# Two large groups of SBUF buffers begin at multiples of 2048 bytes instead of 64-byte ones

## What is computed

```python
def L0(x, d_list, U, Vt, weight, filt, bias):        # U = Vt = adj
    scale = jnp.sum(d_list * filt * d_list, axis=0)
    return U @ (scale[:, None] * (Vt @ (x @ weight))) + bias
def message(X, A, W):
    deg = jnp.sum(A, axis=1, keepdims=True)
    return (A / jnp.where(deg > 0, deg, 1.0)) @ X @ W
def L1(X, A, W_in, W_out):
    return message(X, A, W_in) + message(X, A.T, W_out)
x = layernorm(x + L0(x, ...adj, adj...))
x = layernorm(x + L1(x, adj, W_in, W_out))
```

## Time and profile before

| | |
|---|---|
| median of 3 runs | 762.05 us (761.66 to 762.28) |
| the profiled execution, device time | 761.1 us |
| its span, first to last instruction | 759.3 us |
| granted TensorE clock, mean over the span | 0.997 of full |
| PE busy | 743.7 us (98%), 3346 matmuls |
| DVE busy | 551.8 us (73%) |
| ACT busy | 475.5 us (63%) |
| transferred | 208.64 MB, mean 275 GB/s |

### The profile page before, as it was taken

The page is one execution under the profiler, slowest core; times in us unless marked ns, Lnnn a source line. Parts: engine busy times, 40 slices in busy tenths (PEclk is TensorE's granted clock), DMA queues, the critical chain, the costliest instruction groups (busy, mean ns, idle before and its releaser), DMA issues. The chain is left out here.

```text
span 759.3 us, 9063 instructions
## 1 busy us (share of the span) xinstructions
PE 743.7 (98%) x3346; PEld 605.1 (80%) x3346; DVE 551.8 (73%) x655; ACT 475.5 (63%) x1171; POOL 0.2 (0%) x4
## 2 busy tenths in 40 slices
PE   7999999999999999999999999999999999999995
PEld 4778888888888888788888888888878888888774
DVE  3796956747473464786664647988699988899996
ACT  5796764827264543234333447998799879766673
POOL 0000000000000000000000000000000000000000
PEclk9999999999999999999999999999999999999998
DMA  9988966655555445255455469999989999998980
GB/s 330 409 326 332 357 266 224 255 215 208 215 209 217 163 174 222 83 202 211 169 189 200 169 220 372 381 380 383 382 308 373 382 360 373 379 347 322 347 309 28
DMA packets 35548, 208.64 MB, mean 275 GB/s; under 512 B 3632, under 2 KB 8496, under 8 KB 11056
## 3 DMA queue, kind: packets, MB, share of 16 engines
q1 hardware_dynamic: 35360, 207.99, 72.9%
q10 hardware_dynamic: 144, 0.07, 0.0%
HBM read 205.95 MB, written 2.10 MB: 274 GB/s over the span
## 5 line engine op out<-in xcount | busy, mean ns | idle before, releaser
L371 DVE TENSOR_TENSOR lo<-raw,hi 128x2048 fp32r<-128x2048 f32 x191 | 433.4, 2288 | 151.0 <-ACT hi L271 113.7
L271 ACT ACTIVATE hi<-raw 128x512 fp32r<-128x512 f32 x512 | 315.3, 621 | 51.1 <-DMA raw<-in_adjT_b 32.6
L567 PE MATMUL accA<-hi,x_hi 128*128 128x512 f32 x512 | 203.4, 397 | 3.4 <-ACT hi L271 3.3
L570 PE MATMUL accA<-hi,x_lo 128*128 128x512 f32 x512 | 200.4, 391 | 0.0
L276 ACT ACTIVATE hi<-raw 128x2048 fp32r<-128x2048 f32 x64 | 120.6, 1908 | 62.0 <-DMA raw<-in_adjT_b 61.9
L578 PE MATMUL accA<-lo,x_hi 128*128 128x512 f32 x512 | 139.5, 394 | 0.9 <-DVE lo L371 0.9
L567 PEld LDWEIGHTS accA<-hi,x_hi 128*128 128x128 f32 x512 | 96.2, 188 | 26.0 <-issue 2.4
L578 PEld LDWEIGHTS accA<-lo,x_hi 128*128 128x128 f32 x512 | 95.2, 188 | 25.5 <-DVE lo L371 5.1
L570 PEld LDWEIGHTS accA<-hi,x_lo 128*128 128x128 f32 x512 | 96.3, 188 | 20.2
L567 PE MATMUL accB<-hi,v_hi 128*128 128x512 f32 x256 | 101.2, 395 | 0.9 <-DVE turned L428 0.9
L570 PE MATMUL accB<-hi,v_lo 128*128 128x512 f32 x256 | 100.1, 391 | 0.0
(11 more groups left out here) (66 smaller groups left out, 446.9 us busy)
## 6 DMA issues: line engine op xcount, KB each, us to landing
raw<-in_adjT_b SPq DMA_DIRECT2D x127, 1024.0 KB, 4.9
raw<-in_adj_b SPq DMA_DIRECT2D x64, 1024.0 KB, 6.2
rows<-in_xT_b SPq DMA_DIRECT2D x8, 256.0 KB, 9.7
rows<-in_x_t SPq DMA_DIRECT2D x8, 256.0 KB, 6.1
out<-rows SPq DMA_DIRECT2D x7, 256.0 KB, 8.7
raw<-in_adjT_b SPq DMA_DIRECT2D x4, 256.0 KB, 4.8
out<-rows SPq DMA_DIRECT2D x1, 128.0 KB, 1.8
out<-rows SPq DMA_DIRECT2D x2, 64.0 KB, 2.0
```

The costliest lines, as they stand in the source:

```text
L271: last = nc.scalar.activation(hi[slot][:, t], raw[slot][:, t], ACT.Copy, accum_out=sums[:, TPB * K + t, C:C + 1])
L371: nc.vector.tensor_tensor(lo[slot][:], raw[slot][:], hi[slot][:], ALU.subtract).then_inc(s_lo, 1)
L567: nc.tensor.matmul(acc, r_hi[:, TPB * K + t], h[:, t], start=(first and t == 0), stop=False)
L570: nc.tensor.matmul(acc, r_lo[:, TPB * K + t], h[:, t], start=False, stop=False)
```

## The change

The start of the ring is rounded down to a multiple of 2048 instead of 64, and a filler tensor is put ahead of `x_hi`, so that it starts at a multiple of 2048 too.

```diff
+LINE = 4 * BLK
...
-        ring_at = nc.sbuf_top // 64 * 64 - 2 * RING * CHUNK
+        ring_at = nc.sbuf_top // LINE * LINE - 2 * RING * CHUNK
...
+        pair_at = -(-nc.sbuf_base // LINE) * LINE
+        sb("unused", [P, (pair_at - nc.sbuf_base) // 32 * 8])
         x_hi = sb("x_hi", [P, NT, P], F32R)
```

## The result

The changed kernel takes 756.9 us (median of 6 runs, 756.54 to 758.98), the kernel before beside it 761.76 us (6 runs, 761.12 to 762.28). The ratio is 0.9941, with a 95% interval of 0.9928 to 0.9954: 0.6% faster, 4.9 us, where no change was forecast. The profiled executions have spans of 759.3 and 754.7 us.

A forecast was written before the change was run, and what follows sets the result against it. PE's matmul pace was taken as the bound; moving operands, stationary operands and transfers were each put at 0, so 759.3 + 0 + 0 + 0 = 759.3 us of span, a median of 762.0 us, range 760.0 to 764.0.

The forecast's parts named there:

- What bounds the kernel: PE's pace: 3072 matmuls at 0.229 us plus small ones, 732.4 us; waits and restarts 11.9 us.
- Moving operands: 0: PE's 3072 moving tiles no longer cross a multiple of 2048; bounds 0 and -0.015 us a matmul, 0 taken.
- Stationary operands: 0: Line 567's weight loads: four tile positions, one of them crossing, all last 186 to 192 ns; cost and gain 0.
- Other pace-setters: PE has 111 matmuls in each of two 25 us stretches, neighbours busy or idle; so no contention to relieve.
- The collision rival: Stationary and moving operands at equal positions modulo 2048 hold up 3 of 12 matmuls; 12 us slower, 774 us; 7%.
- The float32r rival: Crossings slow float32r matmuls; without them 0.229 us falls towards 0.214; 716 to 734 us, say 725; 8%.
- Transfers: 0: Quicker landings of chunks in SBUF could bring at most 1.4 us of PE's waits; 0 taken.
- the landing rival: Chunks land quicker, so part of PE's last 1.4 us of waits goes; 760.6 to 762.0 us, say 761.3; 6%.
- The prediction's last sign: If landings shorten by a tenth of a microsecond and PE's waits don't, the 256-byte rule holds and is hidden.
- the rule on pieces of 256 bytes: DMA pieces beginning at a multiple of 256 bytes go in whole transactions; for 8192 bytes 256 beats, not 262, 2.3% less.
- The numbers: Chances for the time: 77% no change; faster beyond 0.2% 12%, within 81%, slower 7%; 17% left outside the range.

The follow-up runs named there:

- the probe: Changed kernel with groups of 24 equal matmuls put ahead, one operand's start shifted from group to group; 226.7 ns a float32r matmul at distance 0, bfloat16 216 ns.

## Why the prediction was wrong

**What bounds the kernel** was right: PE's pace, one large term. The waits and the givebacks are of the size that was read, too.

**Moving operands: 0** is the step that failed, though not in its question: it put a moving tile's address at no cost, and the runs showed 2.2 ns for each of 3072 matmuls, 6.8 us by pace, of which 4.6 came through in the span. It asked only whether an operand crosses a multiple of 2048, and it answered that right: a crossing costs nothing (2720 ns with all tiles crossing, in three layouts). It then let 0 stand for the whole address. The bounds that it gave, 0 and -0.015 us a matmul, contain the true -0.0022; the value taken was the end of them, and the range of the time did not carry them.

**Stationary operands: 0** failed in the same way. The four kinds of tile lie 512 bytes apart, and 512 is a multiple of the 256 that matter. So the trace's "own experiment" held the one thing constant that it should have varied, and its weight loads of 188 ns say nothing of the matmuls beside them: they are 188 ns in every layout.

**Other pace-setters.** "Moving who stands where has no contention to relieve" was drawn from a pace that is the same with busy and idle neighbours. That holds, and excludes DVE, ACT and transfers. It does not exclude PE's own two reads, for the weights and for the moving operand, which are there together in both stretches.

**The collision rival (7%)** had the right pair of readers and the wrong sign. It held that equal positions collide. They are the best, and the old distance of 64 bytes modulo 256 cost 2.2 ns a matmul, those of 128 and 192 bytes 6.0 and 6.7 ns. It also looked at positions modulo 2048, where only a product's first tile of four would be held up, while all 12 matmuls changed their pace. Its argument against itself, DVE's subtraction at equal positions, has one duration and no other distance beside it, so it could not tell.

**The float32r rival (8%)** had the sign and the wrong cause and size: of the 0.015 us over `warm` an address gives back 0.0022. The Trainium skill's "TensorE: Matmul & The Clock Gate", section "Step-by-step: what each phase is for", gives 215.7 ns for a warm matmul of 512 columns; the probe's bfloat16 agrees with 216, and no float32r group of 512 columns came under 226.6. In "SBUF — State Buffer", section "Who interferes with whom", the Trainium skill says that PE never waits on anyone, and in the section on the steps named above, that loading the next tile's weights does not steal read bandwidth from the running matmul. In bfloat16 nothing here speaks against it. In float32r the pace does, 226.7 to 234.1 ns at multiples of 32 bytes by nothing but where the two operands stand, though the reads themselves are not in the trace.

**Transfers: 0** was right, and the landing rival (6%) was half right. The landings of `in_adj_b` did get quicker, from 6.2 to 4.9 us. But the kernel before with its pairs 64 bytes up has the old landings and the new time:

```profile
raw<-in_adj_b SPq DMA_DIRECT2D x64, 1024.0 KB, 6.2
```

and the ring at a multiple of 2048 with the old distance has quick landings (4.8 us) and the old time. So they are worth nothing here. Nor do they follow the ring's address: with the pairs alone moved, the ring stands as before and they take 4.9 us. The prediction's last sign, landings shorter and PE's waits not, came true for these loads, but it does not bear out the rule on pieces of 256 bytes: on the written side the commonest time of an 8192-byte packet is 309 ns in every layout, with the ring 192 bytes behind a multiple of 256 or on one, where 2.3% would be 7 ns.

**The numbers.** The range of 760.0 to 764.0 left 17% outside and the time was there, below. A kernel whose one large term has 3072 members moves by 3 us for each nanosecond; with bounds of 15 ns on each of them, two nanoseconds belonged in the range.

## What to carry to other kernels

Where TensorE is the bound and the operands are float32r, measure its step from start to start, and look at the distance between the moving and the stationary operand's start modulo 256 bytes before looking at either address alone: equal remainders were best for 512 columns (226.7 ns, against 229 to 236), and a 64-byte shift of one group of buffers gave the whole gain. For 256 columns they were not, so measure again for another shape. Shifting one group of buffers alone cost 1.0 and 1.3% here, so a new tensor placed ahead of such a pair can change the time of matmuls that it has nothing to do with. When a term has thousands of members, test the address with a probe of 24 matmuls in each place rather than argue from members that happen to share it.

## What the runs showed of the hardware

PE's float32r step of 512 columns depends on the distance of its two operands' starts in SBUF modulo 256 bytes: 226.7 ns at 0, 229 to 229.8 at 64, 232 to 234 at 32 and from 96 to 224. Two things go beyond the distance: 16 bytes off, it matters which operand moves (236.0 or 233.4 ns), and at 64 bytes one stretch of the kernel ran at 233.3. Behind an interruption the distance 0 has five to nine slower steps before it reaches its pace. The weight load's own time stays 188 ns. bfloat16 has 216 ns at both distances tried. With 256 columns the better of the two distances tried was the other one, 114.2 ns at 192 against 119.7 at 0.

That two reads meet in the memory is the likely reading, and the dependence on their distance speaks for it; the memory's parts were not observed, and no probe left the weight loads out, so the mechanism stays argued. Also open is what makes up the 11 ns between bfloat16 and the best float32r step, by an estimate from these two (3072 x 10.7 ns) 33 us of this kernel.
